# Mixing the values by quarters of the queries, taking the mean on GpSimd and TensorE, and reordering a stack's transfers

## The reference

```python
router_in = hidden_states.mean(axis=1)          # one row of 384 per image
logits = router_in @ Wr + br
_, top_idx = jax.lax.top_k(logits, K)           # K = 6 of 12 heads
...
scores = jnp.einsum('bhqd,bhkd->bhqk', q, k) / jnp.sqrt(jnp.float32(D))
probs = jax.nn.softmax(scores, axis=-1)
ctx = jnp.einsum('bhqk,bhkd->bhqd', probs, v)
...
x = ctx @ Wo + bo + hidden_states               # then a layer norm
```

## Time and profile before

| | |
|---|---|
| median of 3 executions | 3708.58 us (3705.68 to 3709.11) |
| the profiled execution | 3714.32 us, its span 3712.5 us |
| TensorE matmul busy | 3342.9 us (90%) |
| VectorE busy | 2741.3 us (74%) |
| ScalarE busy | 2258.2 us (61%) |
| GpSimd busy | 1399.3 us (38%) |
| granted TensorE clock, mean | 0.946 |

### The profile page before, as it was taken

One profiled execution on the slowest core, in us unless ns is written; L12 is line 12 of the kernel. 1 busy time (PEld: TensorE's weight loads), 2 busy tenths in 40 slices (PEclk: granted clock), 3 DMA queues, 4 the chain that ended last, 5 costly groups with the idle time before them and its releaser, 6 DMA issues. The chain is left out here.

```text
span 3712.5 us, 65162 instructions
## 1 busy us (share of the span) xinstructions
PE 3342.9 (90%) x17998; PEld 1931.1 (52%) x17998; DVE 2741.3 (74%) x5161; ACT 2258.2 (61%) x5369; POOL 1399.3 (38%) x1487
## 2 busy tenths in 40 slices
PE   7969999999999999848999999968888888889887
PEld 4434444444444444437888888844444434434443
DVE  4468888888888888666888888846677677676766
ACT  4334444444444444355777777737877777777785
POOL 2144444444444444272222222210063453443535
PEclk9989999999999999968999999968999999999898
DMA  9999989899989999541000000021222322232221
GB/s 362 369 360 343 333 335 352 315 343 342 346 329 335 343 344 343 224 142 39 17 17 17 17 17 17 17 76 53 64 74 67 91 67 63 80 88 65 54 65 55
DMA packets 230567, 647.35 MB, mean 174 GB/s; under 512 B 31143, under 2 KB 127943, under 8 KB 229959
## 3 DMA queue, kind: packets, MB, share of 16 engines
q0 software_dynamic: 82944, 453.02, 32.5%
q1 hardware_dynamic: 147398, 191.91, 16.5%
HBM read 520.21 MB, written 79.18 MB: 161 GB/s over the span
## 5 line engine op out<-in xcount | busy, mean ns | idle before, releaser
L697 PE MATMUL b_acc<-b_sampled,b_w 128*128 128x512 f32 x2592 | 1211.4, 595 | 0.0
L632 DVE SCALAR_TENSOR_TENSOR b_mix<-shared,b_weight,b_mix 128x384 f32<-128x384 f32 x864 | 531.9, 621 | 140.4 <-ACT b_mix L655 82.9
L697 PEld LDWEIGHTS b_acc<-b_sampled,b_w 128*128 128x128 f32 x2592 | 449.4, 191 | 347.6 <-issue 347.6
L664 ACT ACTIVATE b_sampled<-b_tps 128x384 f32<-128x384 f32 x576 | 282.7, 491 | 566.1 <-PE b_tps L715 549.2
L1966 DVE TENSOR_REDUCE e_neg_top<-e_next 128x1 f32<-128x1024 f32 x384 | 469.4, 1223 | 210.8 <-PE e_next L2276 175.0
L632 DVE SCALAR_TENSOR_TENSOR b_mix<-b_got,b_weight,b_mix 128x384 f32<-128x384 f32 x864 | 530.9, 619 | 93.8 <-ACT b_mix L655 56.8
L2120 ACT ACTIVATE e_unused<-e_next,e_neg_top 128x1024 bf16<-128x1024 f32 x384 | 429.8, 1119 | 125.6 <-DVE e_neg_top L1966 113.2
L2135 ACT ACTIVATE e_prob<-e_s 128x512 f32<-128x512 f32 x768 | 417.1, 598 | 137.6 <-PE e_s L2288 135.2
L588 POOL DMA_INDIRECT shared<-corner_table,b_index x288 | 293.8, 1020 | 419.4 <-DVE b_mix L632 322.6
L588 POOL DMA_INDIRECT b_got<-corner_table,b_index x288 | 291.0, 1010 | 360.1 <-DVE b_mix L632 303.6
L715 PEld LDWEIGHTS b_tps<-ident,b_mix 128*128 128x128 f32 x1728 | 223.1, 142 | 372.6 <-issue 328.0
(11 more groups left out here) (221 smaller groups left out, 5315.3 us busy)
## 6 DMA issues: line engine op xcount, KB each, us to landing
corner_table<-y SPq DMA_DIRECT2D x32, 1536.0 KB, 14.8
e_stack<-e_high SPq DMA_DIRECT2D x384, 64.0 KB, 2.0
shared<-in_x SPq DMA_DIRECT2D x8, 1536.0 KB, 10.6
c_x<-in_x SPq DMA_DIRECT2D x16, 768.0 KB, 4.4
tokens<-y SPq DMA_DIRECT2D x64, 192.0 KB, 1.9
e_tok<-tokens SPq DMA_DIRECT2D x8, 1536.0 KB, 7.2
e_stack<-e_low SPq DMA_DIRECT2D x192, 64.0 KB, 2.0
shared<-tokens SPq DMA_DIRECT2D x8, 1536.0 KB, 7.3
```

The costliest lines, as they stand in the source:

```text
L632: ins = nc.vector.scalar_tensor_tensor(dst[:], src[:, q * C:(q + 1) * C], weight[g][:, q, k, i:i + 1], dst[:], ALU.mult, ALU.add)
L664: nc.scalar.activation(sampled[s % 2][:, :, i * P:(i + 1) * P], tps[t % 2][:, 0:C].rearrange("p (o q) -> p o q", q=P), ACT.Copy).then_inc( ...
L697: last = nc.tensor.matmul(acc[g][co][:], w_conv[:, k, ci, co * P:(co + 1) * P], sampled[s % 2][:, ci], start=(k == 0 and ci == 0), stop=(k ...
```

## The change

- `mix` serves one tile: its four matmuls take the four quarters of the queries, 256 columns each, and all eight tiles add up in the same place. It is called at c = 2 (tiles 0 and 1), at c = 3 to 7 (tiles 2 to 6) and at c = 0 of the next head (tile 7). `odd_copy` goes, and `heads_out` becomes four copies of 32x256.
- The mean: GpSimd adds up the eight tiles of h in `normalise` (seven additions of 128x384), TensorE multiplies the sum by a matrix of 1/1024 in a fill `mean` at (1,0), and VectorE copies the result. The three sums and the scaling on VectorE go. The logits move from (1,4) to (1,2), the router's four parts from (1,5), (1,6), (1,7), (2,3) to (1,3), (1,5), (1,6), (1,7).
- The values: one tile in a fill, eight fills instead of four. Where a `turned` falls on the same step, it comes after `v`.
- `stack_up`: the twelve transfers are ordered so that nine (all keys, the first half of the queries) come first and are waited for by tile 0; the last three (the second half of the queries) have a semaphore of their own, for tile 4.

```diff
...
     STACKS = 3
+    EARLY_DMAS, LATE_DMAS = 9, 3
     UNITS = 2 * STEPS
-    PAIRS = STEPS // 2
+    QUARTERS = P // HD
+    QUARTER = PIX // QUARTERS
...
     H_STEPS = [(0, 0), (0, 1), (0, 2), (0, 2), (0, 3), (0, 4), (0, 4), (0, 5)]
-    MEAN_STEPS = [(0, 6), (0, 7), (1, 3)]
-    LOGIT_STEP = (1, 4)
-    ROUTER_STEPS = [(1, 5), (1, 6), (1, 7), (2, 3)]
-    V_STEPS = [(4, 0), (5, 0), (5, 1), (5, 3)]
+    MEAN_STEP = (1, 0)
+    LOGIT_STEP = (1, 2)
+    ROUTER_STEPS = [(1, 3), (1, 5), (1, 6), (1, 7)]
+    V_STEPS = [(3, 5), (4, 0), (4, 5), (5, 0), (5, 1), (5, 3), (5, 4), (5, 5)]
...
-        if tail and c in (2, 4) and s >= 2:
+        late = prep and (s, c) in V_STEPS
+        if tail and c in (2, 4) and s >= 2 and not late:
             out.append(("turned", 2 * (s - 2) + c // 4))
...
+            if (s, c) == MEAN_STEP:
+                out.append(("mean", 0))
...
+        if tail and c in (2, 4) and s >= 2 and late:
+            out.append(("turned", 2 * (s - 2) + c // 4))
...
-    FIRST = ([("h", t) for t in range(TILES)] + [("logit", 0), ("x", 0), ("x", 1)]
-             + [("v", k) for k in range(TILES // 2)] + [("row", 0), ("x", 2)])
+    FIRST = ([("h", t) for t in range(TILES)] + [("mean", 0), ("logit", 0), ("x", 0), ("x", 1)]
+             + [("v", k) for k in range(TILES)] + [("row", 0), ("x", 2)])
...
-        def stacked_count(n, s):
-            return STACK_DMA * (2 * n + s // STACKS + 1)
+        def stacked_count(n, s, dmas=EARLY_DMAS):
+            return 16 * dmas * (2 * n + s // STACKS + 1)
...
-                    for src, places in ((high, ((0, 0), (0, 1), (1, 0), (1, 2))), (low, ((0, 2), (1, 1)))):
-                        if src is low:
-                            sp.wait_ge(split_done, g + 1)
-                            sp.nop(nofuse=True)
-                        for w, at in places:
-                            for f in range(2):
-                                part = slice(HD * (2 * w + f), HD * (2 * w + f + 1))
-                                sp.dma_start(
-                                    stack[k][HD * at:HD * (at + 1), w, f * HALF:(f + 1) * HALF].bitcast(F32),
-                                    src[part].bitcast(F32)).then_inc(stacked[k], 16)
+                    def put(src, w, at, f):
+                        part = slice(HD * (2 * w + f), HD * (2 * w + f + 1))
+                        sp.dma_start(stack[k][HD * at:HD * (at + 1), w, f * HALF:(f + 1) * HALF].bitcast(F32),
+                                     src[part].bitcast(F32)).then_inc((stacked_late if (w, f) == (0, 1) else stacked)[k],
+                                                                      16)
+                    for at in (0, 2):
+                        for f in range(2):
+                            put(high, 1, at, f)
+                    for at in (0, 1):
+                        put(high, 0, at, 0)
+                    sp.wait_ge(split_done, g + 1)
+                    sp.nop(nofuse=True)
+                    for w, f in ((1, 0), (1, 1), (0, 0), (0, 1)):
+                        put(low, w, 2 - w, f)
+                    for at in (0, 1):
+                        put(high, 0, at, 1)
...
+                    if t >= 2:
+                        pool.wait_ge(summed, (TILES - 1) * n + max(1, t - 2))
+                    elif not isinstance(n, int) or n:
+                        pool.wait_ge(summed, (TILES - 1) * n)
                     pool.nop(nofuse=True)
                     nc.gpsimd.tensor_scalar(h[t % 2][:], tok[:, t], img_rstd[:, t:t + 1], img_shift[:, t:t + 1],
                                             ALU.mult, ALU.add).then_inc(h_ready, 1)
+                    if t:
+                        pool.wait_ge(h_ready, TILES * n + t + 1)
+                        if t == 1 and (not isinstance(n, int) or n):
+                            pool.wait_ge(mean_ready, n)
+                        elif t >= 2:
+                            pool.wait_ge(summed, (TILES - 1) * n + t - 1)
+                        nc.gpsimd.tensor_tensor(h_sum[:], h[0][:] if t == 1 else h_sum[:], h[t % 2][:],
+                                                ALU.add).then_inc(summed, 1)
...
-                def mean(n, u, count, o):
-                    dve.wait_ge(z_free, count.of(("h", TILES - 1)) + 1)
-                    nc.vector.reduce_sum(mean_h[:, o:o + 1], h_t[u][:, o], AX.X).then_inc(rchain, 1)
-                    if o == CH - 1:
-                        dve.wait_ge(rchain, CH * (n + 1))
-                        nc.vector.tensor_scalar(mean_b[:], mean_h[:].unsqueeze(2).to_broadcast([P, CH, P]), 1.0 / PIX,
-                                                None, ALU.mult).then_inc(mean_ready, 1)
...
+                    if kind == "mean":
+                        dve.wait_ge(z_full, count.of(fill))
+                        nc.vector.tensor_copy(mean_b[:], b_z[:, 0:C].rearrange("p (o q) -> p o q", q=P)).then_inc(
+                            mean_ready, 1)
+                        dve.wait_ge(mean_ready, n + 1)
+                        dve.sem_inc(z_free, 1)
                         return
...
-                        nc.vector.tensor_tensor(
-                            v[u][:, 2 * k:2 * k + 2],
-                            b_z[:, 0:2 * WIDE].rearrange("p (t s d) -> p t s d", t=2, d=HD),
-                            w_kept[u][:, :, BV_AT:BQK_AT].unsqueeze(1).to_broadcast([P, 2, KEPT, HD]),
-                            ALU.add).then_inc(z_free, 1)
+                        nc.vector.tensor_tensor(v[u][:, k], b_z[:, 0:WIDE].rearrange("p (s d) -> p s d", d=HD),
+                                                w_kept[u][:, :, BV_AT:BQK_AT], ALU.add).then_inc(z_free, 1)
...
-                    dve.wait_ge(odd_out, g + 1)
-                    for f in range(2):
-                        last = nc.vector.tensor_tensor(ctx[u][to, s // 3, f * HALF:(f + 1) * HALF],
-                                                       odd[HD * (2 + f):HD * (3 + f)], b_acc[HD * f:HD * (f + 1)],
-                                                       ALU.add)
+                    dve.wait_ge(tile_used, STEPS * (g + 1) + 4)
+                    for i in range(QUARTERS):
+                        last = nc.vector.tensor_copy(ctx[u][to, s // 3, i * QUARTER:(i + 1) * QUARTER],
+                                                     b_acc[HD * i:HD * (i + 1), 0:QUARTER])
                     last.then_inc(acc_free, 1)
...
-                            if prep and (s, c) in MEAN_STEPS:
-                                mean(n + 1, 1 - u, count, MEAN_STEPS.index((s, c)))
                             if prep and (s, c) in ROUTER_STEPS:
                                 router(n + 1, 1 - u, ROUTER_STEPS.index((s, c)))
...
                         act.wait_ge(stacked[(s - 1) % STACKS], stacked_count(n, s - 1))
+                        act.wait_ge(stacked_late[(s - 1) % STACKS], stacked_count(n, s - 1, LATE_DMAS))
...
-                        if c % 2 == 0 and f == 0:
-                            act.wait_ge(pair_used, PAIRS * head(n, s) + c // 2 + 1)
+                        if f == 0:
+                            act.wait_ge(tile_used, STEPS * head(n, s) + c + 1)
                         act.wait_ge(s_psum, i + 1)
                         nc.scalar.activation(prob[(2 * c + f) % 8][:], b_s[f][:], ACT.Exp).then_inc(prob_ready, 1)
-                def odd_copy(n, s):
-                    g = head(n, s)
-                    act.wait_ge(pair_used, PAIRS * (g + 1) + 2)
-                    act.wait_ge(acc_free, g + 1)
-                    nc.scalar.activation(odd[2 * HD:], b_acc[2 * HD:], ACT.Copy).then_inc(odd_out, 1)
...
-                            if c == 1 and (s or tail):
-                                odd_copy(*((n, s - 1) if s else (n - 1, KEPT - 1)))
...
+                    elif kind == "mean":
+                        pe.wait_ge(summed, (TILES - 1) * (n + 1))
+                        for o in range(CH):
+                            last = nc.tensor.matmul(b_z[:, o * P:(o + 1) * P], h_sum[:, o * P:(o + 1) * P], share[:],
+                                                    start=True, stop=True)
...
-                        for i in range(2):
-                            t = 2 * k + i
-                            for ci in range(CH):
-                                cols = (2 * CH + ci) * HD
-                                last = nc.tensor.matmul(b_z[:, i * WIDE:(i + 1) * WIDE], h_t[u][:, ci, t * P:(t + 1) * P],
-                                                        w_kept[u][:, :, cols:cols + HD], start=(ci == 0),
-                                                        stop=(ci == CH - 1))
+                        for ci in range(CH):
+                            cols = (2 * CH + ci) * HD
+                            last = nc.tensor.matmul(b_z[:, 0:WIDE], h_t[u][:, ci, k * P:(k + 1) * P],
+                                                    w_kept[u][:, :, cols:cols + HD], start=(ci == 0),
```

(74 more changed lines are left out.)

3 lines of the change are left out of this document (1 added, 2 removed).

## The result

The changed kernel takes 3722.47 us in the median (3709.46 to 3731.08), the kernel before 3709.11 us beside it (3703.24 to 3715.59), 15 executions each. The ratio is 1.0034, with a 95% interval of 1.0027 to 1.0042. So it is slower by a third of a percent, where I had forecast a gain of 0.8%. The profiled execution of the changed kernel has a span of 3729.2 us, 16.7 more than before. It was the slowest of the fifteen, and the profiled execution of the kernel before lay above its median too, by 5.2 us.

The account below looks back on a forecast made before the run. TensorE was taken as the fullest engine, with about 15 us of waits an image and a lowered clock. Six middle images -21 us, first -4, last -7, start +4, last mix and copies -1: -29, median 3680 us, range 3640 to 3725.

Parts of the forecast that it names:

- What bounds the kernel: TensorE is the fullest engine; what can be won is in waits and lowered clock, mostly in heads 2 and 3.
- Order of the stack: Tile 0 waits for nine transfers instead of twelve: -3.0 us a middle image, about 1.1 each at heads 1 and 4.
- Router and weights sooner: Weight loads 3.5 us earlier, residual no longer late at (3,2): -4.0 us; VectorE relieved at (2,3): -3.0 us an image.
- Mixing by tiles: Two or three new occasions on TensorE a head, 0.15 to 0.2 us each: +0.5 us a head, +3.0 an image.
- The mean: Six more TensorE instructions at (1,0): +1.0 us an image; uncovered GpSimd additions before the first image: +4 us once.
- Values one tile at a time: Fills ahead of scores wait 0.3 to 0.5 us each, (4,0) and (5,0) shorten by 1.05: net +1.0 us an image.
- What gives some back: Where TensorE's waits go, VectorE (18.8 of 20.87 us in head 1) or ScalarE is next: +1.5 us an image.
- Slower: Rival, chance 0.19: small mixes cost TensorE in every head and the clock falls at three more places; about 3733 us.
- waits only move: Rival of no change, chance 0.10: VectorE or ScalarE holds each step as before; 3703 to 3712 us.

Follow-up runs that it names:

- late scaling: GpSimd's scaling of the next image's weights moved from step (2,4) to (3,1), behind finish and residual; alone on the kernel before: 3687.9 us, ratio 0.9950.
- stack_mean: The kernel before with the new order of the stack's transfers and the new mean and router, scaling still at (2,4): 3677.1 us, ratio 0.9922.
- v_only: The kernel before with only the values made one tile at a time, eight fills at the new steps: 3725.3 us, ratio 1.0054.

## Why the prediction was wrong

*What bounds the kernel.* TensorE, with waits in heads 2 and 3: right. The version without the stall in head 3 and with the earlier router takes 1071.9 us for the eight images instead of 1137.8, with TensorE's busy time down by 44.5 us and the clock in image 3 at 1.00 from head 1 on.

*Order of the stack.* I took -3.0 us a middle image, -7 in the first and about -5 in the last, some 30 in all. The stack's order alone gives -2.1 a middle image, -9.8 in the first and -3.3 in the last; the whole is 28 us between the profiled executions, but only 17 to 18 by the ratio and the medians. Two readings were wrong. At (4,3) I put 1.1 us down to the stack, but the step lasts as long (3.64 us) when the wait for the stack is gone; TensorE waits there 1.17 us for the bank, in image 3 of both kernels. At (1,3) the wait does go, and later steps of head 1 take it back.

*Router and weights sooner: the step that failed.* I split it in two. The part in head 2 was right and even too small: with the mean and router alone head 2 falls by 4.5 us, from 27.1 to 22.5, against 3.0. The part in head 3, -4.0 us, has the wrong sign: +1.5 with mean and router alone, +1.8 in the whole change (of which the fills of values and the mixing have a part: (3,2) grows by 1.2 us, (3,4) by 0.9 and (3,5) by 0.7). I moved the weights up by 3.5 us against a TensorE that I left where it was. But the same change takes over 3 us out of head 2, and the chain of `high`, twelve transfers, a store, six loads, scaling, finish and residual starts with head 2 and does not get shorter with it. Of my 3.5 us the loads got 2.7, counted from the start of head 2 (12.3 us instead of 15.0), and the scaling and the residual 2.2, while TensorE began to wait 2.9 us sooner. Measured with the mean and router alone, the step was wrong by 4.0 + 1.5 = 5.5 us an image, 33 us in six. The runs with and without the late scaling show that the chain on GpSimd is what holds head 3: 25 us between stack_mean and the same with late scaling, 17 to 20 on the changed kernel, 17 on the kernel before.

*Mixing by tiles.* I said 0.5 us a head, 24 in all; measured 0.47 a head in the middle images and 18 us in all. Right in size, and by a reason that was half right: 0.21 us for splitting a pair, within reach of my 0.15 to 0.2, and beside it a rest of 7 to 9 us that I had set at 0. I had the duration of the copies right (1.73 us, forecast 1.65) and their place wrong: TensorE meets them at the first mix of a head and waits. How much of the rest is theirs is not shown.

The Trainium skill (TensorEngine Tiling (Array Packing), Instruction Overhead) gives about 60 cycles for each matmul, from which I had estimated 0.8 us a head. The sixteen and the eight instructions take the same time, so here the measurement decides against adding that overhead to each of four column tiles side by side at 256 columns. The Trainium skill (TensorEngine Tiling (Array Packing), Key Properties) also states a drain at a change of mode, and gives no price. The 0.21 us for splitting a pair are in line with it, but no run shows that they are the drain.

*The mean.* I took 1.0 us for step (1,0); it grew from 2.14 to 3.51 with the mean, so 1.4. The logits' fill at (1,2) adds 0.9 us, and (1,3) and (1,4) give 1.4 back. GpSimd's additions delay no transpose that I can see. The start costs 5.7 us instead of 4; with the late scaling, the values alone have 2.9 of it.

*Values one tile at a time: the second step that failed.* I took a wait of 0.3 to 0.5 us for each fill ahead of the scores; at (4,5) of image 3 it is 1.25 us in v_only and 1.68 us in the changed kernel, because VectorE has the statistics and the row to do first. The price is 3.3 us an image with late scaling instead of 1.0, and 13 to 20 us in all instead of 6.

*What gives some back.* +1.5 us for VectorE in head 1: head 1 is longer by 1.7 us in the whole change and by 1.5 with the mean alone, but by the mean's and logits' fills in steps 0 and 2, not by VectorE.

*The rivals.* Slower came true, but by 13 us and not by its mechanism: in the middle images head 1 keeps 1.00 and nothing falls at (4,1) or (5,1). Head 4 does lose clock (0.94) in three of the six, but behind the wait of the values' fill at (4,5), 1.68 to 1.69 us, which is the same in the other three, where the clock stays at 1.00. That the time lies just inside my range, up to 3725 us, is luck: the range's upper end belonged to this rival. No rival was the one that happened, the move of the wait to (3,2). I had the "waits only move" case at 0.10, with VectorE and ScalarE as the cause.

*What stays open.* Mixing and values together cost 0.9988 - 0.9859 = 1.29%, 48 us with the late scaling, while they cost 18 and 13 apart. The other 17 us are uncertain by about 11, by my estimate from the four intervals; between the profiled executions they are 13. Of these about 6 lie in the six middle images, most of them in head 3: its clock falls to 0.93 in three of six images (25.0 to 25.1 us against 23.5), and to nothing below 1.00 with one of the two parts alone. By the steps, a fill of values at c = 3, 4 or 5 then shares its step with a mix that used to be elsewhere; I have not tested this by itself. Another 7 us lie in the first image, where heads 1 and 2 have no fill of values. These are heads 1 and 2 of image 0 with mixing and values, then with the mixing alone, both with the late scaling:

```profile
2555.20:2579.73 24.53, 22.27 (x134) 10.73 (x133) 16.21 (x33) 18.50 (x35) 0.00 (x0) 0.79 0.13 34
2579.73:2603.49 23.76, 22.33 (x123) 9.84 (x122) 12.76 (x16) 18.22 (x35) 4.25 (x11) 0.71 0.41 124
```

```profile
2554.78:2575.65 20.87, 18.65 (x134) 9.04 (x133) 16.21 (x33) 18.02 (x35) 0.00 (x0) 1.00 0.16 40
2575.65:2595.79 20.14, 18.67 (x122) 8.27 (x121) 12.76 (x16) 17.80 (x35) 2.14 (x2) 0.92 0.35 95
```

TensorE has the same work in both and waits the same 1.2 and 1.1 us for the copies in steps (1,2) and (2,2). Behind the first wait three steps run at half clock in the one and none in the other. Why is open.

## What to carry to other kernels

When a change shortens one stretch, read every wait behind it again against the new arrival: a chain that starts with the stretch on other engines has its own length, and what is saved ahead of it can come back as a longer wait, with a lower clock behind it (here 1.5 of 4.5 us). An in-order queue that stands in front of a transfer with work behind it that is needed sooner is worth a look first; here moving one call behind two others gave 17 to 25 us without a single instruction more or less. And a piece of work cut in two cost nothing in streaming here (1.07 us either way), but each piece is one more turn of whatever bank or mode it shares.

## What was not expected of the hardware

Sixteen matmul instructions of 256 columns in four column groups took 1.07 us, eight of 512 took 1.06 to 1.07. One group of eight on its own took 0.64. A copy of 32x256 out of PSUM on VectorE took 0.419 us, 0.75 of the 0.557 us for 128x384. The four matmuls of `out` behind a stall took 2.93 us at a granted clock of 0.50, in the kernel before and in the changed one alike, and 1.45 us where the clock was 1.00. The first line is head 3 of the kernel before ahead of the stall, the second behind it:

```profile
3037.58:3039.03 1.45, 1.45 (x6) 0.91 (x5) 1.42 (x2) 1.40 (x4) 1.37 (x2) 1.00 1.05 384
3045.71:3048.64 2.93, 2.93 (x5) 1.72 (x6) 1.23 (x1) 1.98 (x5) 2.65 (x2) 0.50 0.23 67
```

Where the stall was removed, head 3 had a clock of 1.00 in all six middle images of five kernels. The exceptions are the kernel before with the late scaling (0.92 in one image) and the changed kernel with it (0.93 in three). And waits of the same length did not always have the same end: one of 1.2 us was followed by half clock in one kernel and by the full clock in another, and the one of 1.7 us at (4,5) of the changed kernel by half clock in three of six images.
